# Last block of a gated cross-attention kernel: feed-forward products in the scores' PSUM banks, and a new order in its last step

## The reference

```python
x = x + tanh(g_xattn) * attention(layernorm(x), ctx)      # 16 heads of 32, Wq Wk Wv Wo
x = x + tanh(g_ffn) * ffn(layernorm(x))
# ffn(y): y_prev is y moved down by one token
#   xr = mu_r*y + (1-mu_r)*y_prev ;  xk = mu_k*y + (1-mu_k)*y_prev
#   sigmoid(xr @ W_r.T) * (square(relu(xk @ W_k.T)) @ W_v.T)
```

## Time and profile before

| | us |
|---|---|
| median of 3 runs | 1506.6 (1502.66 to 1508.21) |
| the profiled execution's own time | 1507.09 |
| its span, first to last instruction | 1505.2 |
| TensorE busy | 1399.6 (93%) |
| VectorE, ScalarE, GpSimd busy | 1026.9, 790.6, 590.6 |

### The profile page before, as it was taken

How to read it: one execution, slowest core, us unless ns; L and a number is a source line. 1 busy time by engine, 2 the same in 40 slices (tenths; PEclk the granted TensorE clock), 3 DMA queues, 4 the chain that set the end, 5 groups by cost and what they waited for, 6 DMA issues and landing times.

```text
span 1505.2 us, 28257 instructions
## 1 busy us (share of the span) xinstructions
PE 1399.6 (93%) x9616; PEld 1023.9 (68%) x9616; DVE 1026.9 (68%) x1894; ACT 790.6 (53%) x1444; POOL 590.6 (39%) x807
## 2 busy tenths in 40 slices
PE   7876899999999999999999999999999999999977
PEld 6644677676676767677676767677676767677655
DVE  3466576767777686767767686767767676777642
ACT  3346364655637464654637465564737465563621
POOL 1111353534344352534344353534435343434333
PEclk9978899999999999999999999999999999999989
DMA  5521112121202112121102112121101112120100
GB/s 158 150 71 59 47 43 64 49 69 49 60 17 68 41 56 62 49 69 49 54 23 70 41 56 62 49 69 44 50 24 68 50 49 69 49 62 21 36 29 28
DMA packets 98364, 84.09 MB, mean 56 GB/s; under 512 B 49440, under 2 KB 62752, under 8 KB 98336
## 3 DMA queue, kind: packets, MB, share of 16 engines
q1 hardware_dynamic: 98336, 83.72, 18.6%
HBM read 58.79 MB, written 20.71 MB: 53 GB/s over the span
## 4 chain that ended last, share of the span: by engine, by line
PE 81%; ACT 6%; DVE 6%; issue 3%; SPq 1%; DMA 1%; POOL 1%; ACTq 0%; POOLq 0%; DVEq 0%
PE g_bank L1013 44%; PE g_bank L1188 10%; PE o_bank L1142 6%; PE s_bank L1116 4%; PE d_bank L1148 4%; PE s_bank L1092 3%; ACT s_bank L613 2%; PE s_bank L1126 2%; ACT pq L612 2%; PE s_bank L1013 2%; ACT buf L501 2%; PE o_bank L1019 2%; PE d_bank L1019 2%; PE s_bank L1019 1%; DVE mm L829 1%
## 5 line engine op out<-in xcount | busy, mean ns | idle before, releaser
L829 DVE TENSOR_REDUCE mm<-s_bank 128x3 f32<-128x462 f32 (+1 forms) x384 | 200.2, 578 | 187.1 <-PE s_bank L1092 187.1
L833 DVE TENSOR_TENSOR pq<-s_bank,pq 128x512 f16<-128x512 f32 x320 | 220.2, 688 | 69.6 <-ACT s_bank L613 68.9
L612 ACT ACTIVATE pq<-s_bank 128x512 f16<-128x512 f32 x320 | 192.3, 601 | 97.6 <-PE s_bank L1120 97.6
L1188 PE MATMUL g_bank<-buf,WkT 128*128 128x512 f32 x768 | 201.7, 413 | 38.4 <-DVE buf L738 38.4
L1013 PE MATMUL g_bank<-xnT,WqT 128*128 128x512 f32 x768 | 202.1, 410 | 3.6 <-DVE xnT L817 2.1
L1188 PEld LDWEIGHTS g_bank<-buf,WkT 128*128 128x128 f32 x768 | 143.0, 194 | 84.0 <-DVE buf L738 40.1
L1013 PE MATMUL g_bank<-WvT,buf 128*128 128x512 f32 x768 | 196.8, 400 | 2.2 <-POOL buf L433 2.2
L613 ACT ACTIVATE s_bank<-s_bank 128x512 f32<-128x512 f32 x320 | 194.7, 609 | 0.0
L1013 PE MATMUL g_bank<-WoT,buf 128*128 128x512 f32 x768 | 193.0, 401 | 0.0
L1013 PE MATMUL g_bank<-WrT,buf 128*128 128x512 f32 x768 | 189.7, 396 | 2.3 <-DVE place L855 2.3
L437 POOL TENSOR_TENSOR buf<-place,buf 128x512 fp32r<-128x512 f32 x64 | 82.7, 1292 | 245.8 <-ACT buf L501 245.8
(11 more groups left out here) (121 smaller groups left out, 2138.9 us busy)
## 6 DMA issues: line engine op xcount, KB each, us to landing
xa<-in_x SPq DMA_DIRECT2D x64, 256.0 KB, 3.6
x<-in_x SPq DMA_DIRECT2D x64, 256.0 KB, 2.8
out<-x SPq DMA_DIRECT2D x48, 256.0 KB, 2.0
k_all<-k_scratch SPq DMA_DIRECT2D x16, 256.0 KB, 2.8
k_low<-k_scratch SPq DMA_DIRECT2D x16, 256.0 KB, 2.9
v_main<-v_scratch SPq DMA_DIRECT2D x16, 256.0 KB, 2.8
place<-x SPq DMA_DIRECT2D x16, 256.0 KB, 2.3
out<-place SPq DMA_DIRECT2D x16, 256.0 KB, 2.0
```

Source lines behind the costliest of these rows:

```text
L612: nc.scalar.activation(pq[:, n, HI, :], bank[:, :], ACT.Exp, scale=SCALE).then_inc(p_hi, 1)
L829: nc.vector.reduce_max(maxima, scores, AX.X).then_inc(reduced, 1)
L833: nc.vector.tensor_tensor(pq[:, n, LO, :], score_bank[5 * g + n][:, :], pq[:, n, HI, :], ALU.subtract).then_inc(p_lo, 1)
L1188: ins = nc.tensor.matmul(K_BANK[c][:, :], WkT2[:, s, e, cols(c)], buf3[:, m, e, :], start=(e, n) == (0, 0), stop=(e, n) == (C - 1, len(PRO ...
```

## The change

The last block's tail gets banks of its own: K in g_bank[0], g_bank[1], s_bank[0], s_bank[1]; R in s_bank[2], s_bank[3], g_bank[0], g_bank[1]; V in s_bank[0] to s_bank[3]. TensorE's tail is K(0,1), K(2), K(3), R(0) to R(3), V(0) to V(3). In the last step the order around the last group is head_scores(3), V(14,2), tail_scores(3), values(3), R(14,3), projections 0 to 2, x2 transposes 0, projection 3, x2 transposes 1, then V(14,3) into s_bank[2] with x2 transposes 2 before its third chunk and x2 transposes 3 before its fourth. ScalarE's tanh of R(14,3) stands behind attn_high(3), and VectorE's gated(14,3) behind mix_k(0). In the tail ScalarE does xr_high(0) ahead of the relus, and the last output addition is VectorE's instead of GpSimd's. The diff, cut to its core:

```diff
+        K_END = g_bank + s_bank[0:2]
+        R_END = s_bank[2:4] + g_bank
+        V_END = s_bank
+        V3_END = s_bank[2]
@@ sync, tail
-            for t in range(TT):
+            for t in range(TT - 1):
                 store_out(BLOCKS - 1, t)
+            sp.wait_ge(out_last, 1)
+            sp.dma_start(out_tiles[BLOCKS - 1, TT - 1], kept).then_inc(out_stored[TT - 1], 16)
@@ scalar, step
-                    if ffn:
+                    if ffn and (pre or g < G - 1):
                         tanh_r(i - 1, g)
...
                 attn_high(i, G - 1)
+                if not pre:
+                    tanh_r(i - 1, TT - 1)
@@ scalar, tail
+            xr_high(BLOCKS - 1, 0)
             k_relu(BLOCKS - 1, 0)
             k_relu(BLOCKS - 1, 1)
-            for c in range(C):
+            for c in range(1, C):
                 xr_high(BLOCKS - 1, c)
...
-                tanh_r(BLOCKS - 1, t)
+                tanh_r(BLOCKS - 1, t, R_END)
@@ vector, step
-                elif ffn:
-                    gated(i - 1, TT - 1)
                 residual(i, 0, pre)
...
                 mix_k(i, 0)
-                if pre and ffn:
-                    gated(i - 1, TT - 1)
+                if ffn:
+                    gated(i - 1, TT - 1, V_BANK[TT - 1] if pre else V3_END)
                 mix_k(i, 1)
@@ vector, tail
-                k_relu(last, c)
+                k_relu(last, c, K_END)
             for t in range(TT):
-                gated(last, t)
+                gated(last, t, V_END[t])
+            dve.wait_ge(x1_kept, 16 * BLOCKS)
+            dve.wait_ge(u_ready, BLOCKS * TT)
+            nc.vector.tensor_tensor(kept, th[1], kept, ALU.add).then_inc(out_last, 1)
@@ tensor, project
-                else:
-                    pe.wait_ge(u_ready, i * TT + t - 1)
+                elif t == 0:
+                    pe.wait_ge(u_ready, i * TT - 1)
+                else:
+                    pe.wait_ge(th_ready, i * TT)
@@ tensor, step
                 head_scores(i, 3)
-                if ffn:
+                if ffn and pre:
                     ffn_r(i - 1, 3)
+                elif ffn:
+                    ffn_v(i - 1, 2)
...
                 tail_scores(i, 3)
-                if ffn:
-                    ffn_v(i - 1, 2, pre)
+                if ffn and pre:
+                    ffn_v(i - 1, 2)
...
-                    ffn_v(i - 1, 3, pre)
-                    for t in range(TT):
+                    ffn_r(i - 1, 3)
+                    for t in range(3):
                         project(i, t, pre)
-                    for t in range(TT):
-                        x2_transposed(i, t)
+                    x2_transposed(i, 0)
+                    project(i, 3, pre)
+                    x2_transposed(i, 1)
+                    v_product(i - 1, 3, V3_END, lambda c: x2_transposed(i, c) if c >= 2 else None)
@@ tensor, tail
             ffn_k(BLOCKS - 1, (0, 1), queries=False)
-            ffn_k(BLOCKS - 1, (2,))
-            ffn_k(BLOCKS - 1, (3,))
...
+            for c in (2, 3):
+                ffn_k(BLOCKS - 1, (c,), queries=False, bank=K_END)
+            for t in range(TT):
+                if t == 0:
+                    pe.wait_ge(u_ready, (BLOCKS - 1) * TT)
+                elif t >= 2:
+                    wait_relu(pe, BLOCKS - 1, t - 2)
+                r_product(BLOCKS - 1, t, R_END[t])
+            for t in range(TT):
+                if t < 2:
+                    wait_relu(pe, BLOCKS - 1, t + 2)
+                else:
+                    pe.wait_ge(th_ready, (BLOCKS - 1) * TT + t - 1)
+                v_product(BLOCKS - 1, t, V_END[t])
```

More of the change, by code:

```diff
@@ L161, in flamingo_block @@
         relu_ready = [sem("relu01_ready"), sem("relu23_ready")]
+        out_last = sem("out_last")
         r_done, th_ready, v_done, u_ready, out_ready = (sem(n) for n in ("r_done", "th_ready", "v_done", "u_ready", "out_ready"))
@@ L613, in exps, with tanh_r @@
                 nc.scalar.activation(bank[:, :], bank[:, :], ACT.Exp, scale=SCALE).then_inc(p_full, 1)
-            def tanh_r(i, t):
+            def tanh_r(i, t, bank=R_BANK):
                 act.wait_ge(r_done, i * TT + t + 1)
@@ L622, in tanh_r @@
                     act.wait_ge(xr_mixed, i * C + 1)
-                nc.scalar.activation(th[t % 2], R_BANK[t][:, :], ACT.Tanh, scale=0.5).then_inc(th_ready, 1)
+                nc.scalar.activation(th[t % 2], bank[t][:, :], ACT.Tanh, scale=0.5).then_inc(th_ready, 1)
             def attn_high(i, g):
@@ L693, in step @@
                     exps(i, g, 4)
-                    if ffn:
+                    if ffn and (pre or g < G - 1):
                         tanh_r(i - 1, g)
-                    else:
+                    elif not ffn:
                         for u in late_units(1 + g):
@@ L850, in attend, with k_relu, gated @@
                 nc.vector.tensor_tensor(attn32, o_bank[:, :], attn32, ALU.mult).then_inc(attn32_ready, 1)
-            def k_relu(i, c):
+            def k_relu(i, c, bank=K_BANK):
                 dve.wait_ge(k_done, i * C + c + 1)
                 dve.wait_ge(k2_lo, i * C + c - 1)
-                nc.vector.tensor_scalar(k2[c % 2], K_BANK[c][:, :], 0.0, None, ALU.max).then_inc(relu_ready[1], 1)
-            def gated(i, t):
+                nc.vector.tensor_scalar(k2[c % 2], bank[c][:, :], 0.0, None, ALU.max).then_inc(relu_ready[1], 1)
+            def gated(i, t, bank):
                 dve.wait_ge(th_ready, i * TT + t + 1)
                 dve.wait_ge(v_done, i * TT + t + 1)
-                nc.vector.scalar_tensor_tensor(th[t % 2], th[t % 2], 1.0, V_BANK[t][:, :], ALU.add, ALU.mult).then_inc(u_ready, 1)
+                nc.vector.scalar_tensor_tensor(th[t % 2], th[t % 2], 1.0, bank[:, :], ALU.add, ALU.mult).then_inc(u_ready, 1)
             def residual(i, t, pre):
@@ L940, in step @@
                     if ffn and g == 2:
-                        gated(i - 1, 1)
+                        gated(i - 1, 1, V_BANK[1])
                     if pre and g == 3:
@@ L947, in step @@
                     if ffn and g != 2:
-                        gated(i - 1, g - 1)
+                        gated(i - 1, g - 1, V_BANK[g - 1])
                     if not ffn:
@@ L1174, in x2_transposed, with ffn_k @@
                 transposed(x2_bank[t], [xn2[t % 2][:, cols(c)] for c in range(C)]).then_inc(x2_done, 1)
-            def ffn_k(i, columns, queries=True, before=None):
+            def ffn_k(i, columns, queries=True, before=None, bank=K_BANK):
                 if columns == (0, 1) and queries:
                     pe.wait_ge(q_copied, (i + 1) * G + 4)
-                elif columns != (0, 1):
+                elif columns != (0, 1) and queries:
                     wait_relu(pe, i, columns[0] - 2)
@@ L1187, in ffn_k @@
                         for n, (s, m) in enumerate(PRODUCTS):
-                            ins = nc.tensor.matmul(K_BANK[c][:, :], WkT2[:, s, e, cols(c)], buf3[:, m, e, :],
+                            ins = nc.tensor.matmul(bank[c][:, :], WkT2[:, s, e, cols(c)], buf3[:, m, e, :],
                                                    start=(e, n) == (0, 0), stop=(e, n) == (C - 1, len(PRODUCTS) - 1))
@@ L1198, in ffn_r, with r_product, ffn_v @@
                     pe.wait_ge(u_ready, i * TT + t - 1)
[L1199 to L1207, removed]
+                r_product(i, t, R_BANK[t])
+            def r_product(i, t, bank):
+                product(bank[:, :], lambda s, c: buf2[:, s, c, cols(t)], lambda m, c: WrT[:, m, c, :], C,
+                        (lambda c: pe.wait_ge(xr_lo, (i + 1) * C) if c == 0 else None) if t == 0 else None).then_inc(r_done, 1)
+            def ffn_v(i, t, beside=None):
+                if t == TT - 1:
                     pe.wait_ge(x1_ready, (i + 2) * TT)
@@ L1210, in ffn_v, with v_product @@
                     pe.wait_ge(th_ready, i * TT + t + 1)
-                product(V_BANK[t][:, :], lambda s, c: buf1[:, s, c, cols(t)], lambda m, c: WvT2[:, m, c, :], C,
-                        before).then_inc(v_done, 1)
+                v_product(i, t, V_BANK[t], beside)
+            def v_product(i, t, bank, before=None):
+                if t == 0:
+                    pe.wait_ge(k2_lo, (i + 1) * C)
+                product(bank[:, :], lambda s, c: buf1[:, s, c, cols(t)], lambda m, c: WvT2[:, m, c, :], C, before).then_inc(v_done, 1)
             def at(chunk, what):
@@ L1252, in step @@
                 if ffn:
-                    ffn_v(i - 1, 0, pre)
+                    ffn_v(i - 1, 0)
                 else:
@@ L1259, in step @@
                 if ffn:
-                    ffn_v(i - 1, 1, pre)
+                    ffn_v(i - 1, 1)
                 tail_scores(i, 2)
@@ L1311, in step @@
                     if ffn:
-                        ffn_v(i - 1, 3, pre, beside)
+                        ffn_v(i - 1, 3, beside)
                     else:
```

## The result

The median is 1497.18 us over eight runs (1493.83 to 1499.97) against 1506.55 us (1502.66 to 1508.33) over eight of the kernel before: 9.4 us less. The ratio is 0.9940, with a 95% interval of 0.9923 to 0.9956. The forecast was 1498.0 us, faster by over 0.5% with a chance of 0.59; the median lies 0.6% lower, and the interval takes in the 0.5%.

The account below looks back on a forecast made before the run. TensorE, busy 93% of the span, was taken to bound the kernel, with only the last 80 us able to move. 1.8 + 2.27 + 0.46 + 2.21 + 1.74 + 0.65 = 9.1 us off 1507.09 gave 1498.0 us, range 1494.8 to 1501.2.

Parts of the forecast that it names:

- the clock at K: At K(0,1) behind the last step: 8.11 us again, gain 0; bounds 2.3 us less and 0.6 more.
- Own banks for K, R and V: In the tail: the pauses in front of R(0) and V(0) go, 2.27 + 0.46 + 2.21 us, plus 1.74 of clock loss.
- 5.84 more, as before: In the tail: K(0,1) ends at 1464.1 and all K at 1469.95, with no gain in K(2) and K(3).
- even unmoved, at 1470.2, it would cost 0.3: In front of R(0): the last xr_low, expected near 1468.3, would cost 0.3 us if not made earlier.
- x2 transposes between the projections: In the last step: mix_k(0) starts 2.4 us earlier; 1.8 us taken for K's start, bounds 0 to 2.4.
- The gate step's 0.5 us: In VectorE's queue: gated(14,3) between mix_k(0) and mix_k(1) makes it 2.75 us to K instead of 2.26.
- This product fills waits and costs nothing: In the last step: V(14,3) between the x2 transposes costs 0; without that cover it would be 2.8 us.
- C: Before K: V(14,3) keeps TensorE working, the low clock stays away or covers less; up to 2.3 us more gain, 1495.7; chance 0.13.
- The last addition: At the finish: on VectorE, gate product to end of addition falls from 1.40 to 0.72 us; 0.65 us gained, bounds 0.4 and 0.8.
- Rival B: In the new pause at 1427 to 1429.9: the clock falls and costs 1.7 us, total 1499.7; chance 0.35.
- D: The last step's x2 stage gains nothing: K starts at 1457.8, total 1499.8; chance 0.09.
- E: From 1430 through the projections: the clock falls in the new pause and stays low, 10.2 us lost, total 1508.2; chance 0.02.

Follow-up runs that it names:

- e1: The changed kernel with the last step and the last addition put back as before: 1498.53 us, ratio 0.9948 to the kernel before.
- e9: The changed kernel with K(2) and K(3) of the last block in the two old banks, waiting for the relus: 65.54 us from values to the end.
- e7: The changed kernel with ScalarE's xr_high(0) behind the two relus again: 66.28 us from values to the end.
- e6: The changed kernel with the first x2 transposes behind projection 3 again, V(14,3) still among the later ones: 67.41 us from values to the end.
- e4: The changed kernel with the gate step of V(14,3) behind the last xk_low: 64.75 us from values to the end.
- e3: The changed kernel with V(14,3) back ahead of the projections, R(14,3) and V(14,2) in their old places, x2 transposes still interleaved: one run of 1492.48 us.
- e8: The changed kernel with 12 extra matmuls behind V(14,3), in the pause in front of K: 1492.67 us, ratio 0.9912 to the kernel before.
- e5: The changed kernel with the last output addition on GpSimd again: 4.72 us behind V(3) instead of 4.15.
- e12: e11 plus 8 extra matmuls in front of K(0,1) in every loop pass and the last step: 1490.4 us, ratio 0.9893 to the kernel before.
- e2: The changed kernel with the code behind the last step and the last addition put back as before: 1502.22 us, ratio 0.9968 to the kernel before.
- e11: The changed kernel with the edits of e4 and e8 together: 1492.66 us, ratio 0.9902 to the kernel before.

## Why the prediction was right, point by point

The total was right (1498.0 against 1497.18), and so was the sign. In the stages of the profile the sum was 0.9 us short (9.1 against 10.0), mostly by the clock at K. That the total came within 0.8 us is luck in part: the terms that were off leaned both ways, and the eight runs lie 6.1 us apart.

- **Own banks for K, R and V**, 6.68 us forecast, 6.99 measured. Right in mechanism and size, and e1 shows it alone; the 0.3 us more is that rows with no pause between them overlap by 0.16 us, at two places. One sentence was wrong: all K would take "5.84 more, as before" behind K(0,1). It took 5.60, a gain of 0.24 us that the sum had at nothing (e1, and e9 backwards). e7 corrects another: "even unmoved, at 1470.2, it would cost 0.3". It costs 0.96 us. The last xr_low ends where I had placed it, 6.15 us behind K(0,1) (1470.87 in e7), but K(3) ends 0.25 us sooner, and R(0) starts 0.15 us behind that xr_low where it would else overlap K(3)'s end.
- **x2 transposes between the projections**, 2.4 us forecast for mix_k(0), 1.97 measured. The term was mis-sized in its second half: norm2(3) started 15.2 us behind the first projection and not 14.9, with 0.3 us of issue time in front of it in the row at 1447.49. Of what came, 1.5 us are the early first transposes and 0.45 the clock at the last ones (e6). The gate step's 0.5 us came exactly (e4).
- **"This product fills waits and costs nothing"**: true of TensorE, but e3 shows that it also brought nothing, and that with its gate step the old place would be better by 0.36 us from values to the end.
- **The clock at K**, "I let K(0,1) cost its 8.11 again". This step failed: it took 7.31, 0.80 us less. The case was C's, in part. Its reason, more work of TensorE ahead of K, is not shown. Filling the pause removes the low clock altogether (e8); but e3, with V(14,3) away from the transposes, took 7.43, and the profiles that have the changed kernel's work ahead of K spread from 7.22 to 7.38. What goes with the gain is the early transposes: 7.22 to 7.43 in the six profiles that have them and show K(0,1) apart, 7.94 in e6, where the first of them are late, 8.11 before and in e1. Why the low stretch then ends sooner in K stays open. Two readings here were wrong too. The clock fell at 1452.5, some 6 us behind the last projection, and not after 11 us of little work. And the upper bound, "0.6 more (all 24 matmuls at 1.2 GHz)", was too small: 12 of them took 4.99 us at 0.50, so 24 would take 10.0, 1.9 us more.
- **The last addition**, 0.65 forecast, 0.53 measured in the change and 0.57 in e5.
- **Rival B.** Ten of the profiles have the new pause; the clock fell in one, at 1.66 us, near the 1.7 us forecast (e12). The 0.35 that I gave it was too much for these profiles. The pause itself is 2.52 us, not 2.8.
- **Rivals D and E** did not come. K starts 1.5 us earlier, and the longest low stretch of this part in the changed kernel is 3.42 us.

What stays open: what decides whether a pause of 2.2 to 2.5 us makes the clock fall, and where the 5 us between runs of one kernel come from. Every trace has several low stretches in its first 200 us, at places that differ; that they carry the spread was not tried.

## What to carry to other kernels

Where a tail of dependent products waits for a slow chain on another engine, look for idle accumulator banks first: here banks that the scores no longer needed let four products run ahead of the chain, and were worth 7 of the 10 us. Count the clock as part of a pause's price, and ask what stands behind it: a fall was almost free in front of another wait (e2) and cost about half its length in front of dense work (e8). Where a pause cannot be removed, matmuls whose result nobody reads can hold the clock, as long as they end before the real work is released (e8, e11, e12).

## What was not expected of the hardware

The same pause of 2.52 us left the clock at 1.00 in nine profiles and took it to 0.50 in one, with the same code around it. Eight extra matmuls in front of K(0,1), at 15 places, made no pass slower (85.04 to 85.08 us from K to K), and in the one profile of that kernel no fall is left between 210 and 1420 us; each of the other thirteen profiles has two or three there.
